# Linear attention and FFN: denominators and state product as one-head matmul tiles, a slot in another order

## The chip, the cores and the metric

One core of a Trainium2 chip runs the whole kernel. The metric is the device time of one execution in microseconds (us), the median of the runs.

## What is computed

x has 8 batches of 2048 tokens with 512 features; all arithmetic is float32.

```python
q = _split_heads(x @ Wq.T + bq)          # 16 heads of 32
k = _split_heads(x @ Wk.T + bk)
v = _split_heads(x @ Wv.T + bv)
q = jnp.exp(q)
k = jnp.exp(k)
kv = jnp.cumsum(k[:, :, :, None] * v[:, :, None, :], axis=1)
k1 = jnp.cumsum(k, axis=1)
num = jnp.einsum('zsD,zsDd->zsd', q, kv)
den = jnp.sum(q * k1, axis=-1, keepdims=True)
out = num / den                          # heads joined again: out @ Wo.T + bo
x = _layernorm(x + attention(x))
x = _layernorm(x + tanh(((x @ weight) @ aux_weight1) @ aux_weight2 + bias))
```

## The kernel before

The work is cut into 128 tiles of 128 tokens (16 per batch, the eight batches in turn, so that tile k belongs to batch k mod 8). Each engine runs its own written-out order: a function `slot(c, k)` per engine, called by `run_slots` once for every tile, first unrolled, then in a loop of eight slots, then unrolled again. Engines meet by semaphores alone, and each engine takes its instructions strictly in the order in which its `slot` writes them. There is no scheduler.

The three FFN weights are multiplied into one matrix (WfH, WfL) at the start. Each weight and each activation is split into a high and a low part of the faster fp32r type, and `three_pass` makes a product from 12 matmuls of 512 columns: four chunks, each high x high, high x low, low x high. Q and K are projected four tiles at a time (a quad): slot k projects block k mod 4 of Q and K for the next quad, with the features on the partitions, and ScalarE writes exp into QT and KT (L539, L551).

For a tile of tokens the kernel forms the scores of all 16 heads with 16 matmuls of 32 rows (L378), one head each, into the four banks of SC; ScalarE copies them to A (L518), GpSimd masks them (L754). The numerators are, per head, V times the masked scores (L390) plus the state before this tile times Q. The state is a 32 x 32 matrix per head and batch; ScalarE lays it out as a block-diagonal 128 x 128 matrix per group of four heads (stateB, L546), and four full-array fp32 matmuls multiply it with Q (L365). The new part of the state comes from 16 small matmuls of K (token-major, through DRAM: KS, k_rows, Ktok) and V (L402), which VectorE adds (L661). For the denominators VectorE scans K along the tokens (L704), multiplies with Q (L713), ScalarE and GpSimd split the product into qk1H and qk1L (L556, L776), and two full matmuls with a block-diagonal matrix of ones (blockonesR, L411, L412) sum over each head. VectorE takes the reciprocal (L678) and in the next slot multiplies the numerators (L657). ScalarE and GpSimd split the result into oH and oL (L528, L764) for the output projection; VectorE adds the residual (L718), takes the statistics (L720, L722), GpSimd the power -0.5 (L783), VectorE normalises (L730). x1 goes through DRAM (x_rows) to be turned, is split into x1H and x1L (L684, L534, L692) and multiplied with the FFN matrix; then bias (L726), tanh (L559), residual on GpSimd (L787), statistics (L734, L737), normalisation on VectorE (L688) and the store.

TensorE's order in slot k is: state product and scores, then the masked product and the new state of tile k-1, denominators of k, Q and K projections for the quad ahead, output projection of k-1, FFN product of k-2, V of k. PSUM has SC (four banks) and four single banks G0 to G3, each shared by two users:

```python
num_ps, kproj_ps = G[0], G[0]
state_ps, oproj_ps = G[1], G[1]
qproj_ps, ffn_ps = G[2], G[2]
den_ps, v_ps = G[3], G[3]
x1T_ps = SC[:, 0, :]
```

The last four slots have no Q and K projections, since there is no quad ahead, and the last eight tiles update no state.

## Time and profile before

| | |
|---|---|
| median of 3 runs | 2378.44 us (2376.52 to 2379.35) |
| the profiled execution | 2383.27 us, its span 2381.5 us |
| granted TensorE clock, mean | 0.991 of full speed |
| TensorE, VectorE, ScalarE, GpSimd busy | 2294.7, 1837.1, 1036.9, 1332.3 us |
| HBM | 139.99 MB read, 98.57 MB written |

The span runs from the first to the last instruction. A line of the trace names the source line, the engine, the operation, and the output and inputs by their names in the program (G stands for G0 to G3, WK for the buffer that holds y, x1, KS, x1s and qk1). An fp32 matmul is recorded as two passes, so 16 of them show as x32; an fp32r matmul is one. PE is TensorE's matmuls, PEld its weight loads, DVE VectorE, ACT ScalarE, POOL GpSimd, SPq the queue of SyncE, which issues the DMAs. What stands in brackets is idle time of the engine before the instruction, and what ended it.

### The profile page before, as it was taken

What the parts mean: (1) busy time and instruction counts of PE and PEld (TensorE: products, weight loads), DVE (VectorE), ACT (ScalarE), POOL (GpSimd) and SP (SyncE); (2) the same over time, 40 slices, a digit from 0 to 9 for tenths busy, and PEclk for the clock granted to TensorE, in tenths of its full rate; (3) what the DMA queues carried; (4) which work ended last, traced back from release to release, by engine and by line L of the source; (5) the groups of instructions that cost most, each with busy time, mean ns of one, the idle gap of its engine ahead of it and who ended that gap; (6) DMA issues with size and microseconds to landing.
All of it is one profiled execution on the core that took longest, in us unless ns stands there. A gap on an engine that the chain in (4) does not pass through costs nothing. (4 is left out here: it accounts for less than half of the span.)

```text
span 2381.5 us, 58603 instructions
## 1 busy us (share of the span) xinstructions
PE 2294.7 (96%) x21040; PEld 1914.2 (80%) x21040; DVE 1837.1 (77%) x2710; ACT 1036.9 (44%) x2039; POOL 1332.3 (56%) x1669
## 2 busy tenths in 40 slices
PE   3999999999999999999999999999999999999986
PEld 3788888888888888888888888888888888888864
DVE  3588878777878887878878877877878878777764
ACT  2434444444444444444444444444444444444432
POOL 1356556556556556556556566565565565565553
PEclk9999999999999999999999999999999999999988
DMA  6133333333333333333333333333333333333121
GB/s 165 48 109 106 107 107 100 109 104 105 100 107 103 106 104 101 110 101 111 107 97 109 99 106 109 105 101 104 107 99 110 104 104 109 100 101 114 59 63 54
DMA packets 293924, 241.95 MB, mean 102 GB/s; under 512 B 32848, under 2 KB 225360, under 8 KB 293712
## 3 DMA queue, kind: packets, MB, share of 16 engines
q1 hardware_dynamic: 293712, 238.69, 32.7%
q8 instruction: 186, 3.05, 0.6%
q14 instruction: 26, 0.21, 0.0%
HBM read 139.99 MB, written 98.57 MB: 100 GB/s over the span
## 5 line engine op out<-in xcount | busy, mean ns | idle before, releaser
L678 DVE RECIPROCAL o<-G 128x512 f32<-128x512 f32 x128 | 429.8, 3358 | 118.2 <-POOL oL L764 117.1
L776 POOL TENSOR_TENSOR qk1L<-WK,qk1H 128x512 fp32r<-128x512 f32 x128 | 165.2, 1291 | 612.2 <-ACT qk1H L556 612.2
L518 ACT ACTIVATE A<-SC 128x512 f32<-128x512 f32 x512 | 275.5, 592 | 225.7 <-PE G L390 224.8
L754 POOL TENSOR_SCALAR_AFFINE_SELECT A<-A 128x512 f32<-128x512 f32 x512 | 314.5, 640 | 55.3 <-ACT A L518 49.2
L534 ACT ACTIVATE x1H<-SC 128x512 fp32r<-128x512 f32 x128 | 76.8, 600 | 526.4 <-DVE SC L684 526.4
L772 POOL TENSOR_TENSOR xres<-xres,cbc 128x512 f32<-128x512 f32 x128 | 166.1, 1297 | 188.2 <-DMA xres<-x 187.6
L704 DVE TENSOR_TENSOR_SCAN WK<-ones,k,KT 128x128 f32<-128x128 f32 x512 | 213.0, 476 | 51.8 <-ACT KT L551 51.8
L730 DVE TENSOR_SCALAR WK<-xres,mv,rstd 128x512 f32<-128x512 f32 x128 | 187.8, 1467 | 84.1 <-POOL rstd L783 84.1
L311 PE MATMUL G<-WfH,x1H 128*128 128x512 f32 x512 | 204.3, 399 | 28.4 <-DVE x1L L692 20.7
L793 POOL TENSOR_TENSOR xTL<-xin,xTH 128x512 fp32r<-128x512 f32 x128 | 169.4, 1324 | 107.2 <-ACT xTH L569 105.3
L311 PE MATMUL G<-xTH,WqH 128*128 128x512 f32 x512 | 201.8, 394 | 26.5 <-POOL xTL L793 25.9
L311 PE MATMUL G<-WoH,oH 128*128 128x512 f32 x512 | 202.1, 395 | 12.5 <-issue 12.5
L311 PE MATMUL G<-xTH,WkH 128*128 128x512 f32 x512 | 200.3, 391 | 7.6 <-DVE WkL L607 7.6
L313 PE MATMUL G<-WoH,oL 128*128 128x512 f32 x512 | 202.0, 395 | 0.0
L312 PE MATMUL G<-WoL,oH 128*128 128x512 f32 x512 | 202.0, 395 | 0.0
L313 PE MATMUL G<-WfH,x1L 128*128 128x512 f32 x512 | 201.1, 393 | 0.0
L312 PE MATMUL G<-WfL,x1H 128*128 128x512 f32 x512 | 201.1, 393 | 0.0
L313 PE MATMUL G<-xTH,WqL 128*128 128x512 f32 x512 | 200.4, 391 | 0.0
L312 PE MATMUL G<-xTL,WkH 128*128 128x512 f32 x512 | 200.0, 391 | 0.0
L312 PE MATMUL G<-xTL,WqH 128*128 128x512 f32 x512 | 199.9, 390 | 0.0
L313 PE MATMUL G<-xTH,WkL 128*128 128x512 f32 x512 | 199.9, 390 | 0.0
L311 PE MATMUL G<-WvH,xTH 128*128 128x512 f32 x512 | 199.2, 389 | 0.0
(107 smaller groups left out, 5334.6 us busy)
## 6 DMA issues: line engine op xcount, KB each, us to landing
xin<-x SPq DMA_DIRECT2D x512, 64.0 KB, 1.9
xres<-x SPq DMA_DIRECT2D x128, 256.0 KB, 3.0
x_rows<-WK SPq DMA_DIRECT2D x128, 256.0 KB, 2.1
WK<-x_rows SPq DMA_DIRECT2D x512, 64.0 KB, 2.0
out<-WK SPq DMA_DIRECT2D x128, 256.0 KB, 2.1
k_rows<-WK SPq DMA_DIRECT2D x120, 256.0 KB, 3.2
WK<-k_rows SPq DMA_DIRECT2D x480, 64.0 KB, 1.9
QT<-wqT SPq DMA_DIRECT2D x4, 256.0 KB, 4.4
```

Source lines behind the costliest of these rows:

```text
L311: nc.tensor.matmul(out, statH(k), movH(k), start=(k == 0), stop=False)
L312: nc.tensor.matmul(out, statH(k), movL(k), start=False, stop=False)
L313: last = nc.tensor.matmul(out, statL(k), movH(k), start=False, stop=(k == NK - 1))
L518: nc.scalar.activation(A[:, j, :, :].rearrange("p g q -> p (g q)"), SC[:, j, :], ACT.Copy).then_inc(scores_out[j], 1)
L534: nc.scalar.activation(x1H[:, :, :].rearrange("p g q -> p (g q)"), x1T_ps, ACT.Copy).then_inc(x1h_ready, 1)
L678: nc.vector.reciprocal(oflat, den_ps[:, :]).then_inc(recip_ready, 1)
L704: last = nc.vector.tensor_tensor_scan(qk1[:, g, :], ones[:, :].to_broadcast([P, P]), KT[:, nq, g, ncols], k1[:, nb, g:g + 1], ALU.mult, AL ...
L730: nc.vector.tensor_scalar(x1[:, (k - 1) % 2, :], r, mv1[:, 0:1], rstd[:, 0:1], ALU.subtract, ALU.mult).then_inc(x1_ready, 1)
L754: last = nc.gpsimd.affine_select(out=A[:, j, :, :], in_=A[:, j, :, :], compare_op=ALU.is_ge, fill=0.0, base=0, pattern=[[0, NK], [1, P]], ...
L772: nc.gpsimd.tensor_tensor(xres[:, k % 2, :], xres[:, k % 2, :], cbc[:, :], ALU.add).then_inc(xb_ready, 1)
L776: nc.gpsimd.tensor_tensor(qk1L[:, :], WK[:, 7, :], qk1H[:, :].bitcast(F32), ALU.subtract).then_inc(qk1l_ready, 1)
L793: nc.gpsimd.tensor_tensor(halves[1], xin[:, m % XIN, :].rearrange("p (t g q) -> p g t q", t=HG, q=HD), halves[0].bitcast(F32), ALU.subtrac ...
```

## The change

The 128 values of a head's denominators are now made by one matmul per head: a 32 x 32 block of ones (fp32) times the 32 rows of qk1 of that head, no split of qk1. Head (g, j) (group g of four, j in it) uses rows 32j of the array and columns 32g, and its result goes to partitions 32g of SC's bank j. The product of state and Q takes the same 16 tiles straight from `state`; `stateB` and its copies on ScalarE are gone. The masked product of a head goes to the same place, so numerators and denominators lie in the scores' banks, in quarters 0 and 1 of each. The features of o are therefore in another order (chunk j of o holds head j of each of the four groups), and Wo and bv are loaded in that order: Wo by four DMAs, bv by four DMAs of single values in place of one.

A slot is laid out anew: TensorE does scores and V of k, output projection of k-1, denominators, state product and masked product of k (not k-1), new state of k-1, Q and K ahead, FFN product of k-2. The scores wait for o_ready of the tile before. State and K projection share G0, output projection and FFN product G1; Q and V have a bank each. Reciprocal and product with the numerators stand together at the end of VectorE's slot, and the FFN's bias, tanh, residual and second normalisation move to slot k+3. x1 is turned in place in x1s and not into PSUM; x1L is made by GpSimd from x1s. Both normalisations are one ScalarE instruction each, with scale rstd and bias shift = -mean x rstd; GpSimd makes shift with one small instruction more each. On SyncE the load of xin now comes before K's store, and the store of out after both x1 transfers and the load of xres; the x1s load waits for x1l_ready in place of x1_turned.

```diff
+        ones = sb("ones", [P, HD])
...
+        shift = sb("shift", [P, 2])
...
-        num_ps, kproj_ps = G[0], G[0]
-        state_ps, oproj_ps = G[1], G[1]
-        qproj_ps, ffn_ps = G[2], G[2]
-        den_ps, v_ps = G[3], G[3]
-        x1T_ps = SC[:, 0, :]
+        num_ps, den_ps = SC[:, :, 0:P], SC[:, :, P:2 * P]
+        state_ps, kproj_ps = G[0], G[0]
+        oproj_ps, ffn_ps = G[1], G[1]
+        qproj_ps = G[2]
+        v_ps = G[3]
...
                 sp.dma_start(bcol[:, 1, :], bk).then_inc(biases_loaded, 16)
-                sp.dma_start(bcol[:, 2, :], bv).then_inc(biases_loaded, 16)
+                with nc.allow_non_contiguous_dma(reason="512 values in the order of Wo's rows"):
+                    for j in range(HG):
+                        sp.dma_start(bcol[j * HD:(j + 1) * HD, 2, :], bv.rearrange("(f q) a -> a q f", q=HD)[j]
+                                     ).then_inc(biases_loaded, 16)
                 load_by_block(wq_raw, wqT, wq_loaded)
...
-                if c.reads_state(k - 1):
-
-                    wait(pe, k_ready, c.count(k + 4))
-                    wait(pe, stateb_ready, c.count(k - 7))
-                    for g in range(NK):
-                        nc.tensor.matmul(num_ps[:, g * P:(g + 1) * P], stateB[:, g, :], QT[:, ps, g, pcols],
-                                         start=(g == 0), stop=False, skip_group_check=True)
+                heads = [(g, j, slice(g * HD, (g + 1) * HD), slice(j * HD, (j + 1) * HD))
+                         for g in range(NK) for j in range(HG)]
...
-                    for j in range(HG):
-                        wait(pe, scores_out[j], c.count(k))
-                    wait(pe, x1l_ready, c.count(k - 2))
+
+                    wait(pe, o_ready, c.count(k))
...
+                    if not prev:
+                        pe.wait_ge(wvh_ready, 1)
+                        pe.wait_ge(wvl_ready, 1)
+                    wait(pe, v_ready, c.count(k))
+                    three_pass(v_ps[:, :], lambda f: xTH[:, s, f, cols], lambda f: xTL[:, s, f, cols],
+                               lambda f: WvH[:, f, :], lambda f: WvL[:, f, :]).then_inc(v_done, 1)
                 if prev:
...
+                    three_pass(oproj_ps[:, :], lambda f: oH[:, f, :], lambda f: oL[:, f, :],
+                               lambda f: WoH[:, f, :], lambda f: WoL[:, f, :]).then_inc(oproj_done, 1)
+                if att:
+                    wait_before(pe, *[(scores_out[j], c.count(k + 1)) for j in range(HG)],
+                                (qk1_ready, c.count(k + 1)))
+                    for g, j, quarter, h in heads:
+                        last = nc.tensor.matmul(den_ps[quarter, j, :], ones[h, :], qk1[h, g, :], start=True, stop=True)
+                    last.then_inc(den_done, 1)
+                    if c.reads_state(k):
+                        wait_before(pe, (state_ready, c.count(k - 7)))
+                        for g, j, quarter, h in heads:
+                            nc.tensor.matmul(num_ps[quarter, j, :], state[h, k % B, g, :], QT[h, s, g, cols],
+                                             start=True, stop=False, skip_group_check=True)
+                    wait(pe, v_ready, c.count(k + 1))
+                    wait(pe, masked, c.count(k + 1))
+                    for j in range(HG):
+                        for g in range(NK):
                             f0 = g * P + j * HD
-                            last = nc.tensor.matmul(num_ps[h, g * P:(g + 1) * P], V[:, (k - 1) % 2, f0:f0 + HD],
-                                                    A[:, j, g, :], start=(g == 0 and not c.reads_state(k - 1)),
-                                                    stop=True, skip_group_check=True)
+                            last = nc.tensor.matmul(num_ps[g * HD:(g + 1) * HD, j, :], V[:, k % 2, f0:f0 + HD],
+                                                    A[:, j, g, :], start=not c.reads_state(k), stop=True,
+                                                    skip_group_check=True)
                     last.then_inc(num_done, 1)
...
-                if att:
-                    wait(pe, qk1h_ready, c.count(k + 1))
-                    wait(pe, qk1l_ready, c.count(k + 1))
-
-                    wait(pe, v_ready, c.count(k))
-                    nc.tensor.matmul(den_ps[:, :], blockonesR[:], qk1H[:, :], start=True, stop=False)
-                    nc.tensor.matmul(den_ps[:, :], blockonesR[:], qk1L[:, :], start=False,
-                                     stop=True).then_inc(den_done, 1)
...
+                if prev:
+                    n = k - 1
+                    wait(act, shift1_ready, c.count(n + 1))
+                    wait(act, y_ready, c.count(n - 1))
+                    nc.scalar.activation(x1[:, n % 2, :], xres[:, n % 2, :], ACT.Identity, bias=shift[:, 0:1],
+                                         scale=rstd[:, 0:1]).then_inc(x1_ready, 1)
...
+                if fin:
+                    n = k - 3
+                    wait(act, shift2_ready, c.count(n + 1))
+                    nc.scalar.activation(y[:, n % 2, :], y[:, n % 2, :], ACT.Identity, bias=shift[:, 1:2],
+                                         scale=rstd[:, 1:2]).then_inc(out_ready, 1)
+                if att:
+                    wait(act, o_ready, c.count(k + 1))
+                    wait(act, oproj_done, c.count(k))
+                    nc.scalar.activation(oH[:, :, :], o[:, :, :], ACT.Copy).then_inc(oh_ready, 1)
...
+                if c.updates_state(k - 1):
+                    wait(dve, state_done, c.count(k))
+                    sflat = state[:, (k - 1) % B, :, :].rearrange("p g d -> p (g d)")
+                    nc.vector.tensor_tensor(sflat, state_ps[:, 0:NK * HD], sflat, ALU.add).then_inc(state_ready, 1)
+                if att:
+
+                    wait(dve, num_done, c.count(k + 1))
+                    wait(dve, oh_ready, c.count(k))
+                    wait(dve, ol_ready, c.count(k))
+                    nc.vector.reciprocal(o[:, :, :], den_ps).then_inc(recip_ready, 1)
+                    wait(dve, recip_ready, c.count(k + 1))
+                    nc.vector.tensor_tensor(o[:, :, :], num_ps, o[:, :, :], ALU.mult).then_inc(o_ready, 1)
...
+                if ffn:
+                    wait(pool, x1h_ready, c.count(k - 1))
+                    halves = [t[:, :, :].rearrange("p g (t q) -> p g t q", q=HD) for t in (x1H, x1L)]
+                    nc.gpsimd.tensor_tensor(halves[1], x1s[:, :].rearrange("p (t g q) -> p g t q", t=HG, q=HD),
+                                            halves[0].bitcast(F32), ALU.subtract).then_inc(x1l_ready, 1)
...
+                    wait_before(pool, (rstd1_ready, c.count(k)))
+                    nc.gpsimd.tensor_scalar(shift[:, 0:1], mv1[:, 0:1], rstd[:, 0:1], -1.0, ALU.mult,
+                                            ALU.mult).then_inc(shift1_ready, 1)
```

On TensorE, in the loop of eight slots, the part with the small matmuls stood so before (a three_pass product for V ends just before it and Q's begins behind it; the name in front of `<-` is the output, behind it the moving and the stationary operand):

```order
L313 MATMUL G<-WvH,xTL 128x512
L365 MATMUL G<-QT,stateB 128x128 x4
L378 MATMUL SC<-QT,KT 128x128 x16
L390 MATMUL G<-A,V 32x128 x16
L402 MATMUL G<-V,WK 32x32 x16
L411 MATMUL G<-qk1H,blockonesR 128x512
L412 MATMUL G<-qk1L,blockonesR 128x512
L311 MATMUL G<-xTH,WqH 128x512
```

and so in the changed kernel (V's and the output projection's 12 rows each are cut to their first or last):

```order
L367 MATMUL SC<-QT,KT 128x128 x16
L310 MATMUL G<-WvH,xTH 128x512
...
L312 MATMUL G<-WvH,xTL 128x512
L310 MATMUL G<-WoH,oH 128x512
...
L312 MATMUL G<-WoH,oL 128x512
L390 MATMUL SC<-WK,ones 32x128 x16
L395 MATMUL SC<-QT,state 32x128 x16
L402 MATMUL SC<-A,V 32x128 x16
L414 MATMUL G<-V,WK 32x32 x16
L310 MATMUL G<-xTH,WqH 128x512
```

The scores are now cut off from the other small matmuls by two full products, and two groups of 16 take the place of the rows of stateB and blockonesR.

VectorE's slot, before, from the product with the numerators of k-1 to the residual (SC, xres and G are PSUM or SBUF buffers by name, k is k1):

```order
L657 TENSOR_TENSOR o<-G,o 128x512
L661 TENSOR_TENSOR state<-G,state 128x128
L666 STREAM_TRANSPOSE WK<-KT 128x4x4x32
L673 STREAM_TRANSPOSE xin<-xin 128x512
L678 RECIPROCAL o<-G 128x512
L684 STREAM_TRANSPOSE SC<-WK 128x512
L688 TENSOR_SCALAR WK<-WK,mv,rstd 128x512
L692 TENSOR_TENSOR x1L<-SC,x1H 128x512
L704 SCALAR_TENSOR_TENSOR WK<-ones,k,KT 128x128 x4
L710 COPY k<-WK 128x4
L713 TENSOR_TENSOR WK<-WK,QT 128x512
L718 TENSOR_TENSOR xres<-G,xres 128x512
```

and in the changed kernel, from the product of the scanned K with Q to the end of the slot:

```order
L640 TENSOR_TENSOR WK<-WK,QT 128x512
L645 STREAM_TRANSPOSE WK<-WK 128x512
L648 STREAM_TRANSPOSE WK<-KT 128x4x4x32
L655 STREAM_TRANSPOSE xin<-xin 128x512
L658 BN_STATS bnst<-WK 128x6
L661 BN_AGGR mv<-bnst 128x2
L665 TENSOR_TENSOR xres<-G,xres 128x512
L667 BN_STATS bnst<-xres 128x6
L669 BN_AGGR mv<-bnst 128x2
L673 TENSOR_TENSOR state<-G,state 128x128
L679 RECIPROCAL o<-SC 128x512
L681 TENSOR_TENSOR o<-SC,o 128x512
```

Reciprocal and product are neighbours at the end; the TENSOR_SCALAR row of L688 and the subtraction for x1L are gone from between them and the scans, and the scans (L632, ahead of the first row here) now belong to tile k and not k+1. The other normalisation, L730 before, stands nowhere in this queue either.

## Rows read from the trace of the kernel before

**Rows 1.** The page, busy time, share of the span and instructions of each engine.
```profile
PE 2294.7 (96%) x21040; PEld 1914.2 (80%) x21040; DVE 1837.1 (77%) x2710; ACT 1036.9 (44%) x2039; POOL 1332.3 (56%) x1669
```

**Rows 2.** Busy time by stretch: from:to, length, each engine's busy us, granted clock, DMA.
```profile
88.28:215.08 126.80, 126.01 (x1174) 103.03 (x1174) 100.50 (x146) 52.08 (x94) 75.52 (x93) 1.00 0.34 103
215.08:2276.90 2061.82, 2047.00 (x19162) 1716.99 (x19162) 1643.50 (x2425) 928.04 (x1854) 1204.14 (x1506) 1.00 0.34 103
...
2276.90:2330.90 54.00, 42.52 (x331) 33.03 (x330) 39.17 (x55) 19.57 (x41) 28.60 (x38) 0.87 0.19 59
2330.90:2381.50 50.60, 27.85 (x179) 21.09 (x178) 20.48 (x33) 8.71 (x17) 14.85 (x23) 0.79 0.17 57
```

**Rows 3.** Timeline of TensorE, small matmuls of one slot: start, length, what.
```profile
1210.53 1.05 PE L365 MATMUL G<-QT,stateB 128*128 128x128 f32 x8
1211.52 1.17 PE L378 MATMUL SC<-QT,KT 32*128 32x128 f32 x32
1212.62 1.08 PE L390 MATMUL G<-A,V 128*32 128x128 f32 x32
1213.52 0.48 PE L402 MATMUL G<-V,WK 128*32 128x32 f32 x32
1213.92 0.51 PE L411 MATMUL G<-qk1H,blockonesR 128*128 128x512 f32 x1
1214.27 0.39 PE L412 MATMUL G<-qk1L,blockonesR 128*128 128x512 f32 x1
1214.49 0.41 PE L311 MATMUL G<-xTH,WqH 128*128 128x512 f32 x1
```

**Rows 4.** The same view: a three-pass product's start and the next's; two slots' starts.
```profile
1202.37 0.39 PE L311 MATMUL G<-WoH,oH 128*128 128x512 f32 x1
...
1205.09 0.39 PE L311 MATMUL G<-WfH,x1H 128*128 128x512 f32 x1
...
1229.73 1.05 PE L365 MATMUL G<-QT,stateB 128*128 128x128 f32 x8
...
1247.31 1.05 PE L365 MATMUL G<-QT,stateB 128*128 128x128 f32 x8
```

**Rows 5.** The same view: TensorE's wait inside the slot that begins at 1210.53.
```profile
1224.16 0.47 PE L311 MATMUL G<-WfH,x1H 128*128 128x512 f32 x1 [1.31 <-DVE x1L L692]
```

**Rows 6.** The same view, an early slot: V's last matmul and the scores behind it.
```profile
98.90 0.39 PE L313 MATMUL G<-WvH,xTL 128*128 128x512 f32 x1
99.22 1.17 PE L378 MATMUL SC<-QT,KT 32*128 32x128 f32 x32
```

**Rows 7.** Groups by line: busy us, mean ns of one, idle before and its releaser.
```profile
L678 DVE RECIPROCAL o<-G 128x512 f32<-128x512 f32 x128 | 429.8, 3358 | 118.2 <-POOL oL L764 117.1
...
L704 DVE TENSOR_TENSOR_SCAN WK<-ones,k,KT 128x128 f32<-128x128 f32 x512 | 213.0, 476 | 51.8 <-ACT KT L551 51.8
L730 DVE TENSOR_SCALAR WK<-xres,mv,rstd 128x512 f32<-128x512 f32 x128 | 187.8, 1467 | 84.1 <-POOL rstd L783 84.1
...
L518 ACT ACTIVATE A<-SC 128x512 f32<-128x512 f32 x512 | 275.5, 592 | 225.7 <-PE G L390 224.8
L754 POOL TENSOR_SCALAR_AFFINE_SELECT A<-A 128x512 f32<-128x512 f32 x512 | 314.5, 640 | 55.3 <-ACT A L518 49.2
...
L657 DVE TENSOR_TENSOR o<-G,o 128x512 f32<-128x512 f32 x128 | 88.6, 692 | 130.2 <-PE G L390 116.7 <-issue 13.2
...
L787 POOL TENSOR_TENSOR WK<-WK 128x512 f32<-128x512 f32 x128 | 166.0, 1297 | 29.1 <-ACT WK L559 18.8
L783 POOL TENSOR_TENSOR rstd<-ve,mhalf 128x1 f32<-128x1 f32 x128 | 72.6, 567 | 10.7
```

**Rows 8.** SyncE's queue at the start; the page's line on x1's store, us to landing.
```profile
10.42 0.43 SPq L247 DMA_DIRECT2D bcol<-bv  x1
...
x_rows<-WK SPq DMA_DIRECT2D x128, 256.0 KB, 2.1
```

**Rows 9.** Timeline of the end: what ends the waits of reciprocal and FFN product.
```profile
2300.55 3.36 DVE L678 RECIPROCAL o<-G 128x512 f32<-128x512 f32 x1 [2.14 <-POOL oL L764]
...
2305.97 0.76 PE L311 MATMUL G<-WfH,x1H 128*128 128x512 f32 x1 [2.47 <-ACT x1H L534]
```

350 lines of the change are left out of this document (125 added, 225 removed).

## The prediction

> **What bounds the kernel now.** I read the page first: TensorE is busy for 96% of the span, VectorE 77%, ScalarE 44%, GpSimd 56% [rows 1]. A busy share says nothing of what a busy engine is busy with, so I read four stretches next [rows 2]: 8 slots of filling (126.80 us), 116 full slots (2061.82), the distance of the last three slots' scores (54.00) and what comes behind the last scores (50.60). Up to 2276.90 the clock is full and TensorE runs nearly all the time. In the last two stretches it runs 42.5 of 54 and 27.9 of 50.6 us, at a clock share of 0.87 and 0.79. So two things can give time: TensorE's own work in a full slot, and the chain of waits at the end.
>
> TensorE's timeline prices a slot [rows 3]: the product of stateB starts at 1210.53, the scores at 1211.52, the masked product at 1212.62, the new state at 1213.52, the denominators at 1213.92, the Q projection at 1214.49. That is 0.99, 1.10, 0.90, 0.40 and 0.57 us. Each of the five three-pass products takes 2.72 (1202.37 to 1205.09), and one slot without a wait is 17.58 (1229.73 to 1247.31) [rows 4]. 5 x 2.72 + 3.96 is 17.56; 0.02 is rest. The slot before that one took 19.20: in it TensorE waited 1.31 us for x1L on VectorE [rows 5]. 116 slots at 17.58, less 1.2 for three that update no state (0.40 each), are 2038; measured are 2061.8. So some 23 us of such waits lie in the full slots.
>
> **The change on TensorE.** It takes away the products of stateB (0.99) and blockonesR (0.57), 1.56 in all. It adds 16 matmuls for the denominators and 16 for the state, each 32 rows by 32 columns, 128 moving columns, fp32. None such is in the trace. From below: 16 matmuls with 32 moving columns take 0.40, which here is not streaming but issue. From above: 16 with the same 128 columns, which run four side by side, take 0.90 (column tiles) or 1.10 (row tiles) [rows 3]. The 32 recorded passes in 0.90 are eight rounds of four, 0.11 each. If all 16 tiles run together it is two rounds, 0.22, and the issue row, 0.40, ends later. I take 0.45 a group, near the lower row, because the 16 operands share no tile; the ends 0.25 and 1.10 are kept.
>
> The order of kinds matters too. Before, a slot crosses from full array to row tiles, to column tiles, and back. Now V and the output projection stand between scores and denominators, so there are five borders. A border into tiles costs 0.09: the last full matmul and the scores behind it start 0.32 apart (98.90, 99.22) instead of 0.23 [rows 6]. The first full matmul after tiles takes 0.35 instead of 0.22, 0.13 more [rows 3]. The Trainium skill, "TensorEngine Tiling (Array Packing)", Key Properties, says that changing the tiling mode drains the engine, and that speaks against this change. By that rule alone, without a price, the gain could be gone; the two rows price such a border at about a tenth of a us, and they set the sum.
>
> The slot now: 13.60 products, 1.10 scores with 0.09 before them, 0.12 on V's first matmul, 0.09 before the denominators, 0.45, 0.45, 0.10 to the column tiles, 0.90, 0.40, 0.12 on Q's first matmul, 0.02 rest: 17.44, or 0.14 less.
>
> **Do the others keep up?** Count from the start of the scores. V ends at 3.9, the output projection at 6.8, denominators 7.2, state product 7.8, masked product 8.7, new state 9.1, Q 11.9, K 14.6, the last product 17.4. VectorE: z 0.2 to 0.9, four scans (0.48 each), copy and product with Q to 3.4, needed at 6.8. Three transposes to 5.4; statistics of y once GpSimd has added it (four score copies of 0.59 from 1.3, masks of 0.64 behind them, an addition of 1.30) at 5.7, to 6.6; the residual and its statistics 6.9 to 8.5; state 9.5; reciprocal 3.36 to 12.9, product 0.69 to 13.6 [rows 7]. The next scores, which overwrite these banks, come at 17.4: 3.8 to spare. oH and oL (0.6, 1.3) are there at 15.5, needed at 21.3. K's exponential ends at 15.5, 1.9 before the next quad reads it. ScalarE loses stateB and qk1H and gains two normalisations of one pass like its copies, together about 8.0 of 17.4; GpSimd swaps qk1L for x1L and gains two operations no longer than its 0.57 power, 11.4. VectorE gets rid of the normalisation that averages 1.47 [rows 7], of the other one and of x1L (some 0.7 each), and goes from 14.4 a slot (1837.1 over 128) to 11.5. x1 at 10.5, one issue (0.35), 2.1 of store [rows 8] and a load of the same size put x1s at 16, one slot ahead of its use at 31.7 (14.3 into the slot after). On SyncE the output store moves behind both x1 transfers and its xin load ahead of K's; K's rows are needed a slot later. So I cost the moves at nothing, and the 23 us of waits go: x1L no longer stands in VectorE's queue behind a normalisation. What is late next is K's exponential, with 1.9.
>
> Full slots: 116 x 17.44 - 1.2 = 2022, against 2061.8: **-40**. First eight: no stateB there before, so seven slots pay borders and denominators in full (+0.38 each), the masked product comes a slot earlier (+0.9), and the eighth saves 0.6: **+3**.
>
> **The end.** Without Q and K a slot is a chain. Before, reciprocal waits for oL, the FFN product for x1H [rows 9], 18.0 a slot on average. Now: masked product done at 8.7, 0.15, reciprocal 3.36, product 0.69, 0.1, next scores at 13.0; TensorE's own work ends at 11.5. 3 x 13.0 against 54.0: **-15**. Behind the last scores: o at 12.9, oL 15.0, output projection 17.7, residual and statistics 19.6, GpSimd's three 21.0, x1 21.6, store and load 27.8, transpose and halves 30.6, last product at half clock (TensorE has idled for ten us by then, as in the old last stretch with its 0.79) 35.9, then 0.7, 0.6, 1.3, 0.9, 1.1, 0.6 and a store: 43.5 against 50.6: **-7**. At the start bv comes in four issues instead of one, 0.43 each, ahead of Wq [rows 8]: **+1.3**.
>
> Sum: -40 + 3 - 15 - 7 + 1.3 = -57.7. The profiled execution took 2383.27, so it would be 2325.6; the median shown, 2378.44, is 4.8 below it, so I forecast **2321**.
>
> **Rivals.**
> Four at a time: if 32x32 tiles gain nothing over row or column tiles, a group takes 0.90. 124 slots with both groups, less four, are some 248 groups: 0.45 x 248 = +112, 2433; at 1.10, 2482. It decides from 0.68 a group on, where the gain is gone. For it: no row shows row and column tiles at once. Against: rows of each alone show four side by side. 0.11, slower.
> A dear border: into and out of the 32x32 kind the array empties for the length of a matmul, 0.39, instead of 0.1: 2 x 0.29 x 124 = +72, 2393. Only the known kinds of border are priced by a row. 0.04, slower.
> A new wait: reciprocal and product now follow the numerator, in the slot's cycle. Over 3.8 us late, each us costs 120. Little delays in VectorE's queue (state sum ahead of the reciprocal) add up to 18 us a slot: 2390; with less, between 2330 and 2370. 0.06.
> All 16 really together: two rounds and no issue bound, 0.25 a group, -0.20 x 248 = -50: 2271. For it: passes of four different tiles already run inside 0.11. Against it: the 0.40 row. 0.08. The Trainium skill, "TensorE: Matmul & The Clock Gate", Measured speedup vs the span model, has 16 tiles take one matmul plus 4 ns for each further tile; that would give this case, and no run here shows it.
> Nothing moves: the new borders and groups eat up what the waits give back. 0.03.
>
> **Numbers.** Forecast 0.68, its own range 2295 to 2350 (0.35 to 0.57 a group). Faster in all: 0.68 + 0.08 + most of the new-wait case 0.04 = 0.80; within 0.2% (what a measurement of this kernel can tell from no change) 0.03; slower 0.11 + 0.04 + 0.02 = 0.17. 2285 to 2375 takes in 0.30 to 0.67 a group and the mild waits; four at a time, the dear border and the fastest case stay outside.
>
> **What would show it.** Right: the denominators' and the state's x32 rows start 0.4 to 0.5 apart from what follows; a full slot 17.4 with no waits on x1L; last scores 13 apart; ScalarE 44%, VectorE some 64%. Wrong: a group of 0.9, a first pass that starts 0.4 behind the output projection, or "PE SC <- DVE o" in the list of waits.

## The result and the profile after

The changed kernel takes **2326.1 us** (median of 4 runs, 2323.81 to 2327.15), the kernel before 2378.89 beside it (4 runs): a ratio of 0.9776, 95% interval 0.9762 to 0.9791, or 52.8 us less. The profiled execution took 2327.15, its span 2325.3.

The page's busy line and the same four stretches, cut at the scores of the same tiles (to compare with [rows 1] and [rows 2]; the columns are those of [rows 2]):

```profile
PE 2263.8 (97%) x27752; PEld 1824.1 (78%) x27752; DVE 1575.0 (68%) x2316; ACT 1024.5 (44%) x1683; POOL 1460.9 (63%) x1925
```

```profile
88.30:215.34 127.04, 126.78 (x1440) 101.53 (x1440) 89.05 (x129) 57.14 (x95) 79.73 (x103) 1.00 0.35 105
215.34:2239.01 2023.67, 2023.67 (x25425) 1635.61 (x25424) 1401.53 (x2077) 908.63 (x1504) 1319.22 (x1736) 1.00 0.34 105
2239.01:2278.44 39.43, 35.38 (x493) 27.56 (x493) 35.41 (x46) 17.57 (x30) 29.44 (x41) 1.00 0.22 72
2278.44:2325.30 46.86, 25.67 (x200) 18.91 (x200) 19.49 (x29) 12.85 (x20) 22.07 (x32) 0.76 0.19 63
```

| stretch | before | after | difference | forecast |
|---|---|---|---|---|
| up to the first scores | 88.28 | 88.30 | 0.0 | +1.3 |
| first eight slots | 126.80 | 127.04 | +0.2 | +3 |
| 116 full slots | 2061.82 | 2023.67 | -38.2 | -40 |
| last three distances of scores | 54.00 | 39.43 | -14.6 | -15 |
| behind the last scores | 50.60 | 46.86 | -3.7 | -7 |
| span | 2381.5 | 2325.3 | -56.2 | -57.7 |

In the full slots TensorE is busy for the whole stretch, 2023.67 of 2023.67: what is left there is its own work and nothing else. TensorE's timeline of one slot, the small matmuls, the first row of each product beside them and the next scores (answers to [rows 3] and [rows 4]; start, length, what):

```profile
1192.69 1.17 PE L367 MATMUL SC<-QT,KT 32*128 32x128 f32 x32
1193.80 0.50 PE L310 MATMUL G<-WvH,xTH 128*128 128x512 f32 x1
...
1199.46 0.50 PE L390 MATMUL SC<-WK,ones 32*32 32x128 f32 x32
1199.78 0.75 PE L395 MATMUL SC<-QT,state 32*32 32x128 f32 x32
1200.46 1.08 PE L402 MATMUL SC<-A,V 128*32 128x128 f32 x32
1201.36 0.48 PE L414 MATMUL G<-V,WK 128*32 128x32 f32 x32
1201.76 0.50 PE L310 MATMUL G<-xTH,WqH 128*128 128x512 f32 x1
...
1210.15 1.17 PE L367 MATMUL SC<-QT,KT 32*128 32x128 f32 x32
```

From start to start: scores 1.11, denominators 0.32, state product 0.68, masked product 0.90, new state 0.40, and the slot 17.46. In an early slot, where the denominators stand alone (no state is read yet), they take 0.43:

```profile
137.64 0.50 PE L390 MATMUL SC<-WK,ones 32*32 32x128 f32 x32
138.07 1.10 PE L402 MATMUL SC<-A,V 128*32 128x128 f32 x32
```

TensorE's waits over the whole run (the list of waits: us in total, times, longest). No x1L stands in it. The first and the third belong to the start (x's low half and K's weights), the second to the last FFN product, the fourth to the scores of the last three slots:

```profile
PE G L310 <- POOL xTL L713: 27.0, 1, 27.0
PE G L310 <- issue: 8.4, 1, 8.4
PE G L310 <- DVE WkL L576: 6.4, 1, 6.4
PE SC L367 <- DVE o L681: 4.1, 3, 1.4
```

The groups by line that answer to [rows 7] (busy us, mean ns of one, idle before):

```profile
L640 DVE TENSOR_TENSOR WK<-WK,QT 128x512 f32<-128x512 f32 x128 | 136.2, 1064 | 4.4
...
L626 DVE TENSOR_TENSOR WK<-G,bfbc 128x512 f32<-128x512 f32 x128 | 88.6, 692 | 505.8 <-PE G L312 505.8
```

VectorE has 4 us of idle time in each slot in one place: ahead of the FFN's bias (L626), the first of its slot. That is the room behind reciprocal and product. Two short waits, 0.57 for GpSimd and 0.36 for the new state in the slot above, stand elsewhere. And the end, TensorE's two products that wait, of the first also the last matmul (to compare with [rows 9]):

```profile
2293.56 0.77 PE L310 MATMUL G<-WoH,oH 128*128 128x512 f32 x1 [3.31 <-POOL oL L746]
...
2298.39 0.63 PE L312 MATMUL G<-WoH,oL 128*128 128x512 f32 x1
...
2311.27 0.76 PE L310 MATMUL G<-WfH,x1H 128*128 128x512 f32 x1 [8.37 <-issue]
```

### The profile page after: what moved, and what is told of

Same layout as the page of the kernel before. It is cut to its first block, busy times and chain, and to the rows that moved or that the text cites. A ratio compares the mean times of both kernels' runs of the same rounds, so it can differ in the third digit from the quotient of the medians.

```text
span 2325.3 us, 70786 instructions
## 1 busy us (share of the span) xinstructions
PE 2263.8 (97%) x27752; PEld 1824.1 (78%) x27752; DVE 1575.0 (68%) x2316; ACT 1024.5 (44%) x1683; POOL 1460.9 (63%) x1925
## 4 chain that ended last, share of the span: by engine, by line
PE 96%; DVE 1%; DMA 1%; ACT 1%; SPq 0%; POOL 0%; issue 0%; POOLq 0%; DVEq 0%; ACTq 0%
PE G L310 27%; PE G L311 25%; PE G L312 25%; PE SC L367 6%; PE SC L402 6%; PE SC L395 3%; PE SC L390 2%; PE G L414 2%; DVE o L679 1%; PE SC L310 0%; PE SC L312 0%; PE SC L311 0%; DMA KT<-wkT 0%; DMA QT<-wqT 0%; SPq L271 0%
## 5 line engine op out<-in xcount | busy, mean ns | idle before, releaser
L700 POOL TENSOR_SCALAR_AFFINE_SELECT A<-A 128x512 f32<-128x512 f32 x512 | 380.8, 776 | 480.4 <-ACT A L501 480.3
L501 ACT ACTIVATE A<-SC 128x512 f32<-128x512 f32 x512 | 264.3, 605 | 390.8 <-PE SC L367 390.8
L626 DVE TENSOR_TENSOR WK<-G,bfbc 128x512 f32<-128x512 f32 x128 | 88.6, 692 | 505.8 <-PE G L312 505.8
L679 DVE RECIPROCAL o<-SC 128x512 f32<-128x512 f32 x128 | 428.6, 3348 | 2.7 <-PE SC L402 2.4
L530 ACT ACTIVATE WK<-xres,shift,rstd 128x512 f32<-128x512 f32 x128 | 104.4, 816 | 463.7 <-POOL shift L727 463.7
L746 POOL TENSOR_TENSOR oL<-o,oH 128x512 fp32r<-128x512 f32 x128 | 165.7, 1294 | 158.5 <-ACT oH L545 158.5
L310 PE MATMUL G<-xTH,WqH 128*128 128x512 f32 x512 | 214.8, 420 | 27.0 <-POOL xTL L713 27.0
L713 POOL TENSOR_TENSOR xTL<-xin,xTH 128x512 fp32r<-128x512 f32 x128 | 163.2, 1276 | 103.2 <-ACT xTH L516 103.2
L310 PE MATMUL G<-WvH,xTH 128*128 128x512 f32 x512 | 214.2, 418 | 0.0
L632 DVE TENSOR_TENSOR_SCAN WK<-ones,k,KT 128x128 f32<-128x128 f32 x512 | 212.0, 477 | 0.0
L311 PE MATMUL G<-WvL,xTH 128*128 128x512 f32 x512 | 200.8, 392 | 0.0
```

Of the source, the lines that this page charges most:

```text
L310: nc.tensor.matmul(out, statH(k), movH(k), start=(k == 0), stop=False)
L311: nc.tensor.matmul(out, statH(k), movL(k), start=False, stop=False)
L501: nc.scalar.activation(A[:, j, :, :].rearrange("p g q -> p (g q)"), SC[:, j, :], ACT.Copy).then_inc(scores_out[j], 1)
L530: nc.scalar.activation(x1[:, n % 2, :], xres[:, n % 2, :], ACT.Identity, bias=shift[:, 0:1], scale=rstd[:, 0:1]).then_inc(x1_ready, 1)
L632: last = nc.vector.tensor_tensor_scan(qk1[:, g, :], ones[:, 0:1].to_broadcast([P, P]), KT[:, s, g, cols], k1[:, k % B, g:g + 1], ALU.mult, ...
L679: nc.vector.reciprocal(o[:, :, :], den_ps).then_inc(recip_ready, 1)
```

## The experiments

The ratios below are each against the kernel before, run beside it. In three kernels (state first, state apart, interleaved) the denominators' matmul with start=True stands between the state product and the masked product that is added to it, on the same partitions of the same bank. These kernels leave the state's part out of the numerators (the third for some of the heads). The instructions are the same in number and shape, so their times can be read.

### State product ahead of the denominators

```diff
-                    for g, j, quarter, h in heads:
-                        last = nc.tensor.matmul(den_ps[quarter, j, :], ones[h, :], qk1[h, g, :], start=True, stop=True)
-                    last.then_inc(den_done, 1)
                     if c.reads_state(k):
                         wait_before(pe, (state_ready, c.count(k - 7)))
...
+                    wait_before(pe, (qk1_ready, c.count(k + 1)))
+                    for g, j, quarter, h in heads:
+                        last = nc.tensor.matmul(den_ps[quarter, j, :], ones[h, :], qk1[h, g, :], start=True, stop=True)
+                    last.then_inc(den_done, 1)
```

> The changed kernel with one edit: the 16 matmuls of state and Q stand before the 16 of the denominators. In the changed kernel the first group took 0.32 us and the second 0.68. Theory (place decides: the first group behind a long product finds its instructions queued, the second doesn't): the state product now takes about 0.32 and the denominators about 0.68, and the time stays at 2326. Rival (operands decide: each state tile is another weight, the ones are all alike): the state product keeps 0.68 and the denominators 0.32 wherever they stand; time also about 2326. The groups' lengths tell the two apart, not the time.

Measured: 2324.11 (2323.63 to 2326.47), ratio 0.9765 [0.9750, 0.9780]. TensorE's timeline:

```profile
1199.67 0.50 PE L391 MATMUL SC<-QT,state 32*32 32x128 f32 x32
1199.98 0.75 PE L395 MATMUL SC<-WK,ones 32*32 32x128 f32 x32
1200.66 1.08 PE L402 MATMUL SC<-A,V 128*32 128x128 f32 x32
```

Now the state product takes 0.31 and the denominators 0.68. The place in the row decides, not the operands: whoever comes second shows the longer time. The time of the kernel is the same.

### One wait ahead of both groups

```diff
-                                (qk1_ready, c.count(k + 1)))
+                                (qk1_ready, c.count(k + 1)), (state_ready, c.count(k - 7)))
...
-                        wait_before(pe, (state_ready, c.count(k - 7)))
```

> The changed kernel with the state's wait moved ahead of the denominators, so that no wait stands between the two groups of 16. Theory (the second group is slow because its instructions are not yet queued): the group stays near 0.68, a few hundredths less, time 2322 to 2326. Rival (the wait between the groups costs the difference of 0.36): the second group falls to about 0.35 and the time by 120 x 0.33 = 40, to 2286.

Measured: 2327.03 (2323.75 to 2328.06), 0.9776 [0.9761, 0.9791]; the two groups again 0.32 and 0.68. The wait between them costs nothing.

### State product between V and the output projection

The group of the state product is moved to behind V's product, so a full product, the output projection, stands between it and the denominators.

> The changed kernel with the state product between V and the output projection, so that a full product stands before each group of 16. Theory: each group takes about 0.32; that saves 0.36 a slot, and two more borders between kinds of tile cost 0.09 + 0.13 = 0.22: -0.14 x 120 = -17, to 2309. Rival 1 (a group of state tiles is slow by itself): 0.68 stays and the borders come on top: +26, to 2352. Rival 2 (the scores are not copied out in time, 3.5 us after the scores start against the group's start at 4.0): a wait on scores_out of up to 0.3 each slot, 2320 to 2345.

Measured: 2336.53 (2335.27 to 2337.29), 0.9814 [0.9800, 0.9827], 10 us above the changed kernel.

```profile
1200.77 0.50 PE L381 MATMUL SC<-QT,state 32*32 32x128 f32 x32
1201.20 0.50 PE L310 MATMUL G<-WoH,oH 128*128 128x512 f32 x1
...
1204.12 0.50 PE L396 MATMUL SC<-WK,ones 32*32 32x128 f32 x32
1204.56 1.10 PE L403 MATMUL SC<-A,V 128*32 128x128 f32 x32
```

Apart, each group takes 0.43 or 0.44, 0.87 in all, 0.13 less than the 1.00 side by side. But the border is paid once more: the output projection takes 2.92 (1201.20 to 1204.12) instead of 2.81, and V 0.09 more than in the changed kernel. A full slot takes 17.53 instead of 17.45 between its scores; over 116 slots that is some 8 of the 10 us, and the last slots grow by the rest. The two borders were priced about right (0.22 forecast, 0.20 measured). What I had wrong is the group: I had taken 0.32 for each when apart, and it is 0.43.

### Denominators and state product interleaved

The two loops become one; in each round a head's denominators and the state product of a head eight places further.

> The changed kernel with the two groups interleaved head by head, the state matmul of a head eight heads away from the denominators' one, all waits ahead. Theory (only about the first 16 matmuls are queued behind a long product, the rest come at their issue pace of 17 ns for each matmul): 0.24 + 0.27 + 0.1 = about 0.6 for all 32 instead of 1.0, -0.4 x 120 = -48, to 2278. Rival (tiles that are visited twice in turn wait for each other): 1.0 or more, 2326 or slower.

Measured: 2325.68 (2323.74 to 2326.34), 0.9770 [0.9755, 0.9785]: no change.

```profile
1199.20 0.29 PE L390 MATMUL SC<-WK,ones 32*32 32x128 f32 x1
...
1199.52 0.37 PE L390 MATMUL SC<-WK,ones 32*32 32x128 f32 x2
...
1200.20 1.08 PE L401 MATMUL SC<-A,V 128*32 128x128 f32 x32
```

The two groups take 1.00 together, as before. My theory fell: with some 16 matmuls queued behind the product and 17 ns for each of the others I had expected 0.6. Half of the 64 passes stand ahead of the row at 1199.52, so the first half takes 0.32 and the second 0.68, as when the groups stood one behind the other: the division goes by the place in the row. The number is the rival's (tiles that are visited twice wait for each other), but that isn't shown: a head's tile comes again after 15 or 17 matmuls here and after 16 in the changed kernel, so this run hardly changes what the rival is about. The next two experiments ask what a group costs.

### Denominators in row tiles

```diff
-                        last = nc.tensor.matmul(den_ps[quarter, j, :], ones[h, :], qk1[h, g, :], start=True, stop=True)
+                        last = nc.tensor.matmul(den_ps[:, j, :], gones[h, g, :], qk1[h, g, :], start=(g == 0),
+                                                stop=(g == NK - 1), skip_group_check=True)
```

> The changed kernel with the denominators in 16 matmuls of 32 rows by 128 columns (ones in the columns of one head of four, zeros in the others, four of them summed in one PSUM tile) in place of 32 rows by 32 columns; same sums. This makes the group run four tiles at a time, as the scores do, while TensorE's place and all else stay. Theory (a full slot follows TensorE one to one): the group takes 1.10 instead of 0.32, so a full slot grows by 0.78 to 18.2, and 120 slots give 2326 + 94 = 2420, range 2405 to 2430. Rival: the 0.32 is mostly issue and dispatch of 16 instructions, equal for both kinds, and the slot grows by under 0.3: 2330 to 2360.

Measured: 2397.76 (2397.65 to 2398.59), 1.0069 [1.0054, 1.0085].

```profile
1217.57 1.17 PE L392 MATMUL SC<-WK,gones 32*128 32x128 f32 x32
1218.67 0.52 PE L398 MATMUL SC<-QT,state 32*32 32x128 f32 x32
1219.12 1.08 PE L405 MATMUL SC<-A,V 128*32 128x128 f32 x32
```

This is the rival "four at a time" of the prediction, built for one of the two groups. The denominators take 1.10, as the scores do. But the state product behind them, unchanged, now takes 0.45 and not 0.68: behind row tiles it stands alone, and alone it costs what the denominators cost alone in the early slot. The pair rose by 0.55 and the slot by 0.56 (1210.80 to 1228.81 between the rows of its scores), and the kernel by 71.7 us, which is 0.56 for each of 128 tiles. So the slot follows TensorE one to one, and my 94 was wrong because I had taken 0.32 for the price of the group that I replaced.

### The same columns in twice the instructions

```diff
-                        last = nc.tensor.matmul(den_ps[quarter, j, :], ones[h, :], qk1[h, g, :], start=True, stop=True)
+                        for t in (slice(0, 64), slice(64, P)):
+                            last = nc.tensor.matmul(den_ps[quarter, j, t], ones[h, :], qk1[h, g, t], start=True, stop=True)
```

> The changed kernel with each of the 16 denominator matmuls as two of 64 moving columns each: the same columns in all, twice the instructions. Theory (the two groups of 32 x 32 tiles are bound by the number of instructions, 28 to 31 ns each, as the 0.448 of the state product behind row tiles and the 0.408 of the new state suggest): 16 more matmuls cost 0.45 to 0.50 in a slot, pitch 17.9 to 17.95, 2380 to 2387. Rival (bound by the columns that stream, or by the change of tiles and the filling of the array): nothing, 2326; in between if both count.

Measured: 2377.45 (2375.35 to 2379.33, 11 runs), 0.9991 [0.9982, 1.0000]; the whole gain is gone.

```profile
1208.06 0.95 PE L391 MATMUL SC<-WK,ones 32*32 32x64 f32 x60
...
1209.45 1.08 PE L403 MATMUL SC<-A,V 128*32 128x128 f32 x32
```

The pair takes 1.39 and not 1.00, with the same columns: 16 instructions more for 0.39, **24 ns each**. An fp32 instruction is two passes, so this is 12 ns a pass. The new state's 16 matmuls of 32 columns take 0.40, 25 ns each, and a group of 16 with 128 columns that stands alone 0.43. So what a group of 32 x 32 tiles costs here goes by the number of its instructions, and hardly by the columns that stream. It isn't the whole price of the pair: 32 at 24 ns are 0.77 of the 1.00. Nor does it hold for groups of 16 in row or column tiles with the same 128 columns, which take 1.10 and 0.90.

### Both normalisations back on VectorE

The two ScalarE instructions are taken out and VectorE gets, between the state's sum and the reciprocal:

```diff
+                if prev:
+                    wait(dve, shift1_ready, c.count(k))
+                    wait(dve, y_ready, c.count(k - 2))
+                    nc.vector.tensor_scalar(x1[:, (k - 1) % 2, :], r, mv1[:, 0:1], rstd[:, 0:1],
+                                            ALU.subtract, ALU.mult).then_inc(x1_ready, 1)
+                if fin:
+                    wait(dve, shift2_ready, c.count(k - 2))
+                    nc.vector.tensor_scalar(yf, yf, mv2[:, 0:1], rstd[:, 1:2],
+                                            ALU.subtract, ALU.mult).then_inc(out_ready, 1)
```

> The changed kernel with both normalisations back on VectorE, ahead of the state's sum and the reciprocal; all else as changed. Theory (the new layout has room): VectorE gets two instructions of 0.5 to 1.5 us each in a slot, 1.2 to 2.5 us together, ahead of a reciprocal whose product had 3.8 us to spare before the next scores. So the full slots stay at 17.45 and only the chain behind the last scores may grow by about 1: 2326 to 2332. Rival (the normalisations' move to ScalarE is what ended the 23 us of waits, whatever the layout): the waits come back, 2346 to 2350, with TensorE waiting for o or for x1 in the full slots.

Measured: **2532.16** (2528.14 to 2546.93), 1.0649 [1.0616, 1.0681], 206 us above the changed kernel. I had forecast nothing. VectorE's timeline in one slot:

```profile
1244.50 0.55 DVE L666 TENSOR_SCALAR WK<-xres,mv,rstd 128x512 f32<-128x512 f32 x1 [2.10 <-POOL shift L725]
1245.94 1.50 DVE L670 TENSOR_SCALAR WK<-WK,mv,rstd 128x512 f32<-128x512 f32 x1 [0.89 <-POOL shift L734]
1247.36 3.34 DVE L677 RECIPROCAL o<-SC 128x512 f32<-128x512 f32 x1
```

I had counted the two lengths, 0.55 and 1.50, against 3.8 us of room. But they stand right behind the statistics that they need, and wait for GpSimd to work on them: 2.10 and 0.89 more. From the end of the state's sum (its row ends at 1242.40) to the reciprocal it is 5.0 us, more than the room. The slots, from scores to scores, now come in turns of four: 17.47, 19.00, 18.79 and 19.94 (1215.10 to 1290.30), 18.8 on average and 1.35 more than in the changed kernel. TensorE's waits for its scores (whole run) and the full slots (columns as in [rows 2]):

```profile
PE SC L367 <- DVE o L679: 98.4, 65, 5.7
PE SC L367 <- ACT KT L538: 74.1, 31, 3.1
```

```profile
228.08:2422.81 2194.73, 2047.93 (x25425) 1650.58 (x25425) 1768.04 (x2310) 719.27 (x1272) 1338.06 (x1737) 0.99 0.32 97
```

So o comes too late for the scores, and once in a quad K's exponential does. That one is ScalarE's and stands behind oH, which waits for the same o; it is what the prediction had named as late next. The full slots take 2194.7 instead of 2023.7, 171 us more; the first eight 13 more, the last three distances of scores 18, the end 3.

### The two kernels between: before, with its normalisations treated otherwise

First the kernel before with one thing moved, y's normalisation from ahead of x1L to behind it:

```diff
-                if fin:
-                    wait(dve, rstd2_ready, c.count(k - 2))
-                    nc.vector.tensor_scalar(yf, yf, mv2[:, 0:1], rstd[:, 1:2],
-                                            ALU.subtract, ALU.mult).then_inc(out_ready, 1)
...
+                if fin:
+                    wait(dve, rstd2_ready, c.count(k - 2))
+                    nc.vector.tensor_scalar(yf, yf, mv2[:, 0:1], rstd[:, 1:2],
+                                            ALU.subtract, ALU.mult).then_inc(out_ready, 1)
```

> The kernel before with one thing moved: on VectorE the normalisation of y (L688) stands behind the subtraction for x1L (L692) instead of ahead of it. Theory: before, TensorE waited for x1L because that normalisation, which took from 0.5 us to 1.6 us where it ran at the same time as GpSimd's addition for xres, stood in front of it. With x1L first, most of the 23 us of waits in the full slots go: 2356 to 2362, and the waits of the FFN product for x1L disappear from the list. Rival: x1L is late for another reason (its transposition or the reciprocal ahead of both), or the wait only passes to the next in the queue: 2374 to 2380.

Measured: 2372.88 (2371.22 to 2373.26), 0.9963 [0.9950, 0.9977], a third of what I expected. The list of TensorE's waits in the full slots, the row on x1L, first of the kernel before, then of this one:

```profile
PE G L311 <- DVE x1L L692: 11.8, 14, 1.3
```

```profile
PE G L311 <- DVE x1L L688: 7.3, 14, 0.8
```

The stretched normalisation was a part of the lateness and not all of it. 14 waits are left, most of them of 0.5 us and none above 0.8.

Then the kernel before with both normalisations on ScalarE, as in the change, and its layout kept:

```diff
+                if prev:
+                    n = k - 1
+                    wait(act, shift1_ready, c.count(n + 1))
+                    wait(act, y_ready, c.count(n - 1))
+                    nc.scalar.activation(x1[:, n % 2, :], xres[:, n % 2, :], ACT.Identity, bias=shift[:, 0:1],
+                                         scale=rstd[:, 0:1]).then_inc(x1_ready, 1)
```

> The kernel before with that part of the change alone: both normalisations on ScalarE with scale and bias, the shift made by GpSimd; layout, denominators and state product as before. Theory: both normalisations leave VectorE's queue, so x1L comes in time and the waits in the full slots go, 23 us less, and nothing else changes: 2354 to 2360. Rival: ScalarE's copies of the scores or GpSimd's masks get delayed instead (the shift and the normalisation stand in their queues), so the masked product is late in some slots: 2370 to 2385.

Measured: **2436.38** (2433.97 to 2438.21), 1.0230 [1.0216, 1.0244], 56 us slower than before. The list of VectorE's waits, of this kernel and then of the kernel before:

```profile
DVE bnst L738 <- POOL WK L794: 317.3, 128, 3.1
DVE o L691 <- POOL oL L768: 200.2, 127, 3.6
```

```profile
DVE o L678 <- POOL oL L764: 117.1, 127, 2.4
...
DVE bnst L734 <- POOL WK L787: 22.9, 18, 2.0
```

VectorE loses two instructions of 1.47 and 0.74 us [rows 7 for the first], and the time comes back as waiting for GpSimd: 2.5 us a slot for the FFN's residual (L794), since the statistics of y had stood behind the normalisation, which filled that time. One of GpSimd's two new instructions stands right ahead of that residual, and its low half of o comes later too. On TensorE most slots take 17.72 to 17.76 instead of 17.58, and in the full slots it waits for x1L 30 times, 18.8 us in all, instead of 14 times and 11.8. Which of these delays makes the 56 us no run separates. So this part of the change, alone, is a loss; in the new layout the same work on VectorE would cost 206 us. What is worth something is the pair.

### Filler ahead of the last two products

```diff
+            def keep_busy(count):
+                for i in range(count):
+                    nc.tensor.matmul(qproj_ps[:, :], WqH[:, i % 4, 0:P], xTH[:, 0, i % 4, :], start=True, stop=True)
...
+                    if not att:
+                        keep_busy(14)
                     wait(pe, oh_ready, c.count(k))
...
+                    if not prev:
+                        keep_busy(34)
                     wait(pe, x1h_ready, c.count(k - 1))
```

> The changed kernel with products that nobody uses (Q's weights times x, into Q's free bank): 14 matmuls ahead of the last output projection and 34 ahead of the last FFN product, where TensorE waits 3.31 and 8.37 us. All else as changed. Theory (the end is 47 us instead of the 43.5 forecast since the last two products behind a pause run at half clock, 6.3 us each instead of 2.8): with TensorE busy ahead of them the granted clock stays full, both take 2.8 to 3, and the time is 6.5 to 7 us shorter: 2319 to 2320. Rival (the two products do not set the end, or the clock falls whatever TensorE does there): 2326, or up to 3 us more if the filler makes the products late.

Measured: **2322.49** (2322.07 to 2322.91, 5 runs), 0.9759 [0.9745, 0.9772], 3.6 below the changed kernel and the fastest of all. The rows of the last products, and the stretch behind the last scores (columns as in [rows 2]):

```profile
2293.84 0.47 PE L310 MATMUL G<-WoH,oH 128*128 128x512 f32 x1 [0.17 <-issue]
...
2296.46 0.39 PE L312 MATMUL G<-WoH,oL 128*128 128x512 f32 x1
...
2309.23 0.47 PE L310 MATMUL G<-WfH,x1H 128*128 128x512 f32 x1 [0.33 <-issue]
```

```profile
2278.70:2320.89 42.19, 31.69 (x248) 24.69 (x248) 19.43 (x29) 12.87 (x20) 22.15 (x32) 0.94 0.22 70
```

The granted clock of the stretch rises from 0.76 to 0.94, the products run at 2.4 GHz and end 2.6 us after their start instead of 4.8 (first to last start of 12), and the stretch takes 42.2 instead of 46.9, some 2.3 less at each of the two products. I had expected 6.5 to 7: I had read 6.3 us as a product's length, which is the distance to the next row, with a wait of 0.88 in it. The Trainium skill, "TensorE: Matmul & The Clock Gate", Wait — 56ns, not 53.3ns?, has a matmul of 512 columns start 426.7 ns after the one before with the array cold and 215.7 ns warm. At half clock the changed kernel's trace agrees with 0.43 (2294.55 to 2294.98); at full clock its fp32r matmuls start 0.227 apart (2.72 for 12), some 5% more than the page has.

### V's product ahead of the last scores, two ways

```diff
+                    ahead = not c.exists(k + 3)
+                    if ahead:
+                        project_v()
                     wait(pe, o_ready, c.count(k))
```

> As the kernel with filler at the end, and in the last three slots V's product stands ahead of the scores, where TensorE waits 1.35 us for o, instead of behind them. Theory (in those slots the chain masked product, reciprocal, product, scores, V, output projection sets the pitch of 13.14; with V out of it TensorE's own 11.8 does): 1.35 less in each of two or three slots, and 2.85 less behind the last scores: 6 to 7 us below the kernel with filler alone, 2312 to 2314. Rival (the copies and masks of the scores are then what the masked product waits for, or the FFN product's x1): 0 to 3 below it, 2317 to 2320.

Measured: 2324.83 (2324.31 to 2325.29), 0.9768 [0.9755, 0.9782], 2.3 slower than with filler alone.

```profile
2261.95 0.47 PE L310 MATMUL G<-WfH,x1H 128*128 128x512 f32 x1 [1.71 <-DVE xres L680]
```

Now the FFN product, which shares its bank with the output projection, waits for VectorE to read that bank (xres), and V stands behind it in TensorE's queue. In the changed kernel's last slots the FFN product had no such wait: it comes later there, when VectorE has read the bank. So in the next kernel V stands ahead of the FFN product too:

```diff
+                if c.exists(k + 1) and not proj:
+                    project_v(c, k + 1)
                 if ffn:
```

> The kernel with filler at the end, and in the last slots V's product for the next tile stands ahead of the FFN product (and so ahead of the next scores), so that V is no longer in the chain from the scores to the masked product and the FFN product does not stand waiting for its bank ahead of V. Theory (VectorE's own queue, from one reciprocal to the next, takes 13.1 us in these slots: 3.36, 0.69, 0.68, 3.25, 0.42, 1.07, 0.70, a wait of 0.56, 0.69, 0.18, 0.69, 0.69, 0.18; so the pitch of 13.15 stays, whatever TensorE does first): 2321 to 2324, no gain over the kernel with filler alone. Rival (only the chain through V sets the pitch): 11.8 to 12 a slot and 2.85 less behind the last scores, 2315 to 2317.

Measured: 2324.91 (2324.41 to 2326.07), 0.9761 [0.9748, 0.9774]: no gain. The distance of these scores stays 13.0:

```profile
2252.95 1.17 PE L378 MATMUL SC<-QT,KT 32*128 32x128 f32 x32
...
2265.95 1.17 PE L378 MATMUL SC<-QT,KT 32*128 32x128 f32 x32 [1.10 <-DVE o L697]
```

TensorE still waits 1.10 for o, the slot ahead of these takes 14.4 instead of 13.15, since it makes two products for V, and the stretch behind the last scores takes 43.6 instead of the 42.2 with filler alone. With V out of the chain the scores are no earlier; that agrees with a queue of VectorE that is 13.1 us long by itself, as its instructions add up in the expectation. No run here shortened that queue.

## Why the prediction came out right, step by step

**The full slot** was forecast at 17.44 and is 17.45 (17.46 between two rows). Its small terms: 1.10 for the scores is 1.10; the borders of 0.12, 0.09 and 0.12 are 0.13, 0.09 and 0.14 (V 2.85, output projection 2.81, Q 2.86 instead of 2.72); denominators, state product and the border to column tiles were 0.45, 0.45 and 0.10, 1.00 in all, and are 0.32 and 0.68, 1.00 in all. The choice of the lower row (16 matmuls in 0.40 "which is not streaming but issue") was right for the reason given: 24 ns an instruction. That the 1.00 is right to the hundredth is in part luck: alone a group takes 0.43 to 0.45 with its border to the column tiles in it, which is 0.87 for two, and the other 0.13 has no explanation here. The division between the two rows that I said would show it (0.4 to 0.5 each) was wrong: the first group's rows start earlier than its share, and the second shows the rest.

Of the 38.2 us in the full slots, some 15 are this work (17.58 to 17.45 in 116 slots), and the other 23 are slots that no longer run over.

**All 16 together** (2271) fell by that price. The rule of the Trainium skill that I had cited for it, "TensorE: Matmul & The Clock Gate", Measured speedup vs the span model, 4 ns for each further tile, isn't what bounds this case. The same page of the Trainium skill, Wait — 56ns, not 53.3ns?, says that starts never come closer than about 25 ns however small the matmul. Taken by whole instructions, the 24 ns of the doubled ones agree with it; the recorded passes start closer, the first of the interleaved kernel 0.01 apart or less. **Four at a time** fell too: the row tiles show what it would have been, 1.10 for a group instead of 0.45. **The dear border** fell: 0.09 to 0.14 each. The Trainium skill, "TensorEngine Tiling (Array Packing)", Key Properties, has a change of the tiling mode drain the engine. The trace agrees in so far as each change costs something, about a tenth of a us; whether the engine drains no run here shows.

**The waits** of 23 us are gone, as forecast, and none took their place: 4.07 us of idle time ahead of L626 in the timeline is the 3.8 that I had counted. The 23 is a difference of slots, and I called all of it waits on x1L. As idle time the full slots before hold 14.8 (2061.82 less 2047.00 in [rows 2]), 11.8 of it for x1L; a slot loses some 0.3 more than the bracket of its wait shows (19.20 less 17.58 is 1.62, the bracket in [rows 5] 1.31). But the experiments show that I had the reason only by half. I wrote that x1L no longer stands behind a normalisation. Moving the normalisation from ahead of x1L in the old kernel gives 8 us of the 23, and taking both normalisations away there costs 56. In the new layout VectorE has 4 us of room in each slot, and with the normalisations in it that room is gone and waits come back; which part of the layout makes the room, no run separates. The rival of a new wait didn't come up in the full slots, but its threshold is borne out by the kernel with the normalisations on VectorE: with 5.0 us put in where there were 3.8, the slots are longer and the whole time with them. "PE SC <- DVE o", my sign of being wrong, does stand in the list of waits, but only three times, in the last slots, where I had counted on o as what the scores wait for. ScalarE is at 44% as forecast, VectorE at 68% and not 64%, in part because the product with Q (L640) got longer.

**The first eight slots** cost 0.2 and not 3. A clean slot there is 16.89, and was 16.71 before: 0.18 more and not 0.38, since the denominators alone take 0.43 with a border in it, where I had charged 0.45 and the border, and since the border of 0.09 ahead of the scores, which I had charged as new, stood in those slots before too [rows 6]. Four of the slots before were 16.79 to 17.00 with small waits, which are gone too, the eighth saves 0.7, and the first slot, where I had put 0.9 for the masked product, grew by 0.6. **The start** cost nothing instead of 1.3: the first scores come at 88.30 instead of 88.28, so bv's load, though it holds back Wq's by 1.0 (issued at 11.88 instead of 10.90), isn't on the chain there.

**The last three slots** are 13.14, forecast 13.0. **The end** is the term that failed: 46.9 instead of 43.5. Up to oL (15.1 behind the last scores, forecast 15.0) all is as forecast. Then the output projection, which I had taken at 2.7, runs at half clock, 5.3 us, after only 3.31 us of waiting: 2.6 of the 3.4. I had given half clock to the last product alone. The kernel before had shown it already: the matmuls of its own last output projection, behind a pause of 2.86, start 0.23 apart at first (2352.22 to 2352.45) and then 0.42 to 0.43.

```profile
2355.08 0.63 PE L312 MATMUL G<-WoL,oH 128*128 128x512 f32 x1
2355.50 0.63 PE L313 MATMUL G<-WoH,oL 128*128 128x512 f32 x1
```

The filler shows it from the other side, with 42.2.

**From the span to the median**: the profiled execution of before lay 4.8 above its median, and I took that off. That of the changed kernel lies 1.05 above its own. This is where most of the 5.1 us between 2321 and 2326.1 comes from; the sum against the span was 1.5 off. That the sum came so close is luck in part: the first eight slots and the start were forecast 4.1 too long, the end 3.4 and the full slots 1.8 too short.

## What to carry to other kernels

Price a group of 32 x 32 matmuls by its instructions first (here 24 to 27 ns each, with 32 to 128 columns), read it as a whole with its neighbours, and add a tenth of a us for each border between kinds of tiles. Before work is moved off an engine whose queue is a loop through others, ask what will stand in its place: a wait for the same partner gives nothing back, and an instruction that is put right behind the statistics that it needs costs the round trip, not its length. At a kernel's end, give a product behind a pause of TensorE of some us (3.31 and 8.37 here; not the 1.35 ahead of the scores) its price at half clock, or keep TensorE busy there.

## What was not expected of the hardware

Two groups of 16 that use the same 32 x 32 tiles take 1.00 side by side and 0.87 with a full product between them. Neither the order of the two, nor the wait, nor interleaving them changes the 1.00. Where the 0.13 goes is open; no run here tells. In the row of a first group 0.32 is not its price: 16 instructions at 24 ns are 0.39 already. Both groups use the same tiles, and whether that is the 0.13 is untested: in none of these kernels does one group use other tiles than the other while both stand side by side.

A product with Q on VectorE (L640, both operands and the result in SBUF) took 692 ns before and 1064 after, the masks on GpSimd 640 [rows 7] and now 776, with no change in either instruction. Both now run beside other instructions than before; what slows them isn't shown. It held up nothing in the full slots, where TensorE doesn't wait.

The output projection at the end ran at half clock after a pause of 3.31 us, while the scores ran at full clock after pauses of 1.35.
